# A graph network with mixtures of experts: gathers written out with their indices read from the table, and the first normalisation inside the stage that builds the masks

## The reference, cut to what matters

```python
x = x + _L0_gnn_ref(_layernorm(x), src, dst, ...)
# in each of two attention layers, 8 heads of 32:
e = sum(q[dst] * k[src]) / sqrt(32);  a = exp(e - segment_max(e, dst)[dst])
agg = segment_sum(v[src] * a / segment_sum(a, dst)[dst], dst)
h = _layer_norm(agg @ Wo + h, g, b)
x = x + _L0_ffn_ref(_layernorm(x)[None], ...)[0]
x = x + _L1_gnn_ref(_layernorm(x), W_self, W_neigh, src, dst)
# summed = segment_sum(h_sparse[src], dst);  h_self + summed / max(deg, 1)
x = x + _L1_ffn_ref(_layernorm(x)[None], ...)[0]
```

## Time and profile before

| | us |
|---|---|
| median of 3 runs | 6103.55 |
| lowest, highest | 6103.26, 6105.42 |
| the profiled execution | 6110.16 |
| its span, first to last instruction | 6108.3 |
| busy PE / DVE / ACT / POOL in the span | 4518.1 / 3914.2 / 2030.2 / 2849.7 |
| mean granted clock of PE, share of full speed | 0.884 |

### The profile page before, as it was taken

How to read it: one execution, slowest core, us unless ns; L and a number is a source line. 1 busy time by engine, 2 the same in 40 slices (tenths; PEclk the granted TensorE clock), 3 DMA queues, 4 the chain that set the end, 5 groups by cost and what they waited for, 6 DMA issues and landing times. The chain is left out here.

```text
span 6108.3 us, 95354 instructions
## 1 busy us (share of the span) xinstructions
PE 4518.1 (74%) x23436; PEld 3415.7 (56%) x23437; DVE 3914.2 (64%) x7196; ACT 2030.2 (33%) x4756; POOL 2849.7 (47%) x2776
## 2 busy tenths in 40 slices
PE   0589999999689999999859679364565656446986
PEld 0466666666476666666659679353443434424553
DVE  4668888888768888888766656795444444732332
ACT  0135555555415555555433223320000000213332
POOL 0057777777017777777300010006777777053332
PEclk9999999999899999999979889696777776557998
DMA  6457666666147666666420040013333333133334
GB/s 92 133 174 200 193 189 191 192 191 183 47 166 203 197 190 191 189 191 191 125 72 0 0 108 0 7 36 94 104 102 104 104 103 103 35 116 89 54 53 82
DMA packets 357896, 732.25 MB, mean 120 GB/s; under 512 B 73235, under 2 KB 205225, under 8 KB 357377
## 3 DMA queue, kind: packets, MB, share of 16 engines
q0 software_dynamic: 194912, 575.52, 34.3%
q1 hardware_dynamic: 162642, 150.27, 9.0%
q10 hardware_dynamic: 80, 3.20, 0.2%
HBM read 627.96 MB, written 107.19 MB: 120 GB/s over the span
## 5 line engine op out<-in xcount | busy, mean ns | idle before, releaser
L973 POOL DMA_INDIRECT rows_a<-kv_scratch,att_idx x848 | 862.5, 1017 | 923.6 <-issue 557.3
L735 POOL DMA_INDIRECT rows_a<-k_scratch,sage_sum_idx x832 | 802.9, 965 | 855.8 <-issue 850.9
L973 POOL DMA_INDIRECT rows_c<-kv_scratch,att_idx x816 | 878.7, 1077 | 268.6 <-issue 243.4
L1431 PE MATMUL ps<-rows_a 128*128 128x258 f32 x1664 | 626.6, 542 | 458.5 <-DMA rows_a<-k_scratch,sage_sum_idx 313.8
L1111 PE MATMUL ps<-attention_rows_b,att_work 128*128 x3328 | 848.0, 395 | 51.7 <-DVE att_work L1219 37.6
L1030 ACT ACTIVATE attention_rows_b<-ps x1664 | 649.3, 390 | 589.6 <-PE ps L1125 413.1
L1431 PEld LDWEIGHTS ps<-rows_a 128*128 128x128 f32 x1664 | 426.0, 268 | 658.7 <-DVE sage_rows_b L1409 394.4
L1409 DVE TENSOR_TENSOR sage_rows_b<-sage_rows_b,ps 128x258 f32 x832 | 353.1, 424 | 569.1 <-PE ps L1431 376.8
L1111 PEld LDWEIGHTS ps<-attention_rows_b,att_work 128*128 128x128 f32 x3328 | 596.6, 192 | 165.0 <-issue 91.2
L1125 PE MATMUL ps<-rows_a,att_work 128*128 128x264 f32 x1696 | 515.7, 431 | 63.2 <-issue 51.1
L1125 PE MATMUL ps<-rows_c,att_work 128*128 128x264 f32 x1632 | 504.8, 430 | 36.0 <-issue 30.2
(11 more groups left out here) (400 smaller groups left out, 9421.6 us busy)
## 6 DMA issues: line engine op xcount, KB each, us to landing
kv_scratch<-rows_c SPq DMA_DIRECT2D x100, 256.0 KB
slot_in<-rows_c SPq DMA_DIRECT2D x1, 13674.0 KB
rows_a<-slot_in SPq DMA_DIRECT2D x106, 129.0 KB
rows_a<-kv_scratch,att_idx POOLq DMA_INDIRECT x848
rows_a<-k_scratch,sage_sum_idx POOLq DMA_INDIRECT x832, 2.8
rows_c<-kv_scratch,att_idx POOLq DMA_INDIRECT x816
h_scratch<-rows_a SPq DMA_DIRECT2D x2, 6400.0 KB
rows_a<-h_scratch SPq DMA_DIRECT2D x50, 256.0 KB
```

What stands on the lines that cost most here:

```text
L735: pool.indirect_dma_start(ring[:, slot, 0:D], None, table, bass.IndirectOffsetOnAxis(ap=idx[:, slot:slot + 1], axis=0)).then_inc(landed[sl ...
L973: pool.indirect_dma_start(r.halves[h][:, u, 0:KV], None, c.kv_dram[:, :], bass.IndirectOffsetOnAxis(ap=idx[:, slot:slot + 1], axis=0)).the ...
L1431: mm = pe.matmul(c.ps[:, to:to + nw], s_buf[:, q, u, :], rhs, start=True, stop=True)
```

## The change

The load of `x` goes into the table stage, on ACT's queue, into `rows_c`. The masks' stage takes the statistics there and writes the normalised rows to `rows_a`; only then are the masks built over `x` in `rows_c`. The chain table is saved from ACT's queue. The masks' save is waited for at the end of the projection, with a semaphore that is held until attention is over; the projection's buffers in `rows_c` move behind the masks. `item_tile` moves to the end of `rows_b`. In attention and in the neighbour sums ACT's copies of indices are gone; POOL's gathers are written out, 104 halves of 8, each half with a wait on PE's count, and take their indices from `src_idx`.

```diff
-def item_tables(c, src, dst):
+def item_tables(c, x, src, dst):
...
+            @block.scalar
+            def _(a):
+                a.wait_ge(loaded, 96)
+                a.wait_ge(zeroed, 1)
+                rows = rows3(c.rows_c)
+                a.dma_start(rows[:, 0:FULL_ROWS // P, :],
+                            x[0:FULL_ROWS, :].rearrange("(t p) d -> p t d", p=P)).then_inc(x_loaded, 16)
+                a.dma_start(rows[0:LAST_ROWS, FULL_ROWS // P, :], x[FULL_ROWS:N, :]).then_inc(x_loaded, 16)
+                a.wait_ge(x_loaded, 32)
...
                 v.memset(st_i, 0).then_inc(padded, 1)
+                v.memset(c.rows_c[:, FULL_ROWS // P * D:NT * D], 0.0).then_inc(zeroed, 1)
...
# qkv
-        used_cols = [0]
+        used_cols = [BLOCKS * MASKW // 2]
...
                 sp.wait_ge(saved, 16)
+                sp.wait_ge(c.masks_saved, 16)
...
# segment_masks, SP
-                sp.wait_ge(zeroed, 1)
-                rows = rows3(c.rows_a)
-                sp.dma_start(rows[:, 0:FULL_ROWS // P, :],
-                             x[0:FULL_ROWS, :].rearrange("(t p) d -> p t d", p=P)).then_inc(x_loaded, 16)
-                sp.dma_start(rows[0:LAST_ROWS, FULL_ROWS // P, :], x[FULL_ROWS:N, :]).then_inc(x_loaded, 16)
                 sp.wait_ge(masked_all, 1)
-                sp.dma_start(c.mask_dram.rearrange("g p e -> p g e"), masks).then_inc(masks_saved, 16)
-                sp.wait_ge(row_ready, 1)
-                sp.dma_start(c.chain_dram.rearrange("(a i) -> a i", a=1), chain.rearrange("p b i -> p (b i)")
-                             ).then_inc(masks_saved, 16)
-                sp.wait_ge(x_loaded, 32)
-                sp.wait_ge(masks_saved, 32)
+                sp.dma_start(c.mask_dram.rearrange("g p e -> p g e"), masks).then_inc(c.masks_saved, 16)
+
+            @block.scalar
+            def _(a):
+                a.wait_ge(var_ready, 1)
+                a.activation(c.rstd[:, :], c.rstd[:, :], ACT.Sqrt).then_inc(rooted, 1)
+                a.wait_ge(scaled, 1)
+
+                def apply(t):
+                    at, col = bass.ds(t * D, D), bass.ds(t, 1)
+                    a.activation(c.rows_a[:, at], c.rows_c[:, at], ACT.Identity, bias=c.nbias[:, col],
+                                 scale=c.rstd[:, col]).then_inc(normed, 1)
+                tiles_of_ten(a, by_vector, NT - by_vector, apply)
+                a.wait_ge(row_ready, 1)
+                a.dma_start(c.chain_dram.rearrange("(a i) -> a i", a=1), chain.rearrange("p b i -> p (b i)")
+                            ).then_inc(chain_saved, 16)
+                a.wait_ge(chain_saved, 16)
...
# segment_masks, DVE
-                v.memset(c.rows_a[:, FULL_ROWS // P * D:NT * D], 0.0).then_inc(zeroed, 1)
...
                 do(v.tensor_scalar(c.head_mask[:, :], c.head_row[:, :], 1.0, BIG, ALU.subtract, ALU.mult))
+                tiles_of_ten(v, 0, NT, lambda t: row_stats(v, c, c.rows_c, t, taken))
+                v.wait_ge(taken, NT)
+                row_scales(v, c, do, var_ready, rooted, scaled)
...
+                tiles_of_ten(v, 0, by_vector, apply)
+                v.wait_ge(applied, by_vector)
+                v.wait_ge(normed, NT - by_vector)
                 v.wait_ge(loaded, 16 * (H + 1))
...
# attention, POOL
-                def fetch(i, h):
-                    pool.wait_ge(staged, i * RING_HALVES + h + 1)
+                for g in range(ITEMS // HALF):
+                    need(pool, summed, 8 * g - 40)
                     pool.sem_inc(gate, 1)
+                    h = g % RING_HALVES
                     for u in range(HALF):
-                        slot = h * HALF + u
+                        item = g * HALF + u
                         pool.indirect_dma_start(r.halves[h][:, u, 0:KV], None, c.kv_dram[:, :],
-                                                bass.IndirectOffsetOnAxis(ap=idx[:, slot:slot + 1], axis=0)
-                                                ).then_inc(landed[slot // BATCH], 16)
-                with pool.Fori(0, ROUNDS) as i:
-                    for h in range(RING_HALVES):
-                        fetch(i, h)
-                for h in range(ITEMS // HALF - ROUNDS * RING_HALVES):
-                    fetch(ROUNDS, h)
+                                                bass.IndirectOffsetOnAxis(ap=c.src_idx[:, item:item + 1], axis=0)
+                                                ).then_inc(landed[(h * HALF + u) // BATCH], 16)
...
# attention, ACT
-                def stage(g, n):
-                    need(a, summed, 8 * g - 40)
-                    a.activation(idx[:, n * HALF:(n + 1) * HALF], c.src_idx[:, bass.ds(g * HALF, HALF)],
-                                 ACT.Copy).then_inc(staged, 1)
...
# edge_sums, POOL (ACT's part is gone)
-                gather_rows(pool, table, ring, idx, staged, gate, landed, weighted)
+                for g in range(ITEMS // HALF):
+                    pool.wait_ge(summed, 2 * g + 2)
+                    pool.sem_inc(gate, 1)
+                    for u in range(HALF):
+                        item = g * HALF + u
+                        pool.indirect_dma_start(ring[:, item % RING, 0:D], None, table,
+                                                bass.IndirectOffsetOnAxis(ap=c.src_idx[:, item:item + 1], axis=0)
+                                                ).then_inc(landed[item % RING], 16)
...
# build
-            segment_masks(c, x)
-            layer_norm(c, c.rows_a, c.rows_a, "ln_in")
+            held = memory.enter_context(Semaphores(nc))
+            c.masks_saved = held.sem("masks_saved")
+            segment_masks(c)
```

More of the change, by code:

```diff
@@ L236, in item_tables @@
     bank_rows = c.rows_a[0:1, o:o + 3 * IC * P].bitcast(I32).rearrange("p (k i) -> p k i", k=3)
-    assert o + 3 * IC * P <= NT * D
+    assert o + 3 * IC * P <= NT * D and at[0] <= (NT + 1) * QW - IC * P
     with Semaphores(nc) as s:
@@ L429, in _ @@
                     v.wait_ge(taken, NT)
[L430 to L448, removed]
+                row_scales(v, c, do, var_ready, rooted, ready, normed_twice)
                 def apply(t):
@@ L773, in segment_masks @@
     with Semaphores(nc) as s:
-        loaded, step, zeroed, x_loaded = (s.sem(n) for n in ("sid_loaded", "mask_step", "pad_zeroed", "x_in_loaded"))
-        masked_all, masks_saved, row_ready, spread = (s.sem(n) for n in ("masked_all", "masks_saved", "cb_row", "cb_spread"))
+        loaded, step, chain_saved = (s.sem(n) for n in ("sid_loaded", "mask_step", "chain_saved"))
+        masked_all, row_ready, spread = (s.sem(n) for n in ("masked_all", "cb_row", "cb_spread"))
+        taken, var_ready, rooted, scaled, applied, normed = (
+            s.sem(f"ln_in_{n}") for n in ("stats", "var", "root", "ready", "applied", "normed"))
         with nc.Block() as block:
@@ L1051, in put_weights @@
                     a.activation(r.rescale, c.ps[:, X_PS + 384:X_PS + 384 + H], ACT.Copy).then_inc(r_ready, 1)
-                for h in range(RING_HALVES):
-                    stage(h, h)
                 for b in range(5):
@@ L1077, in phase @@
                             keep(g)
-                        if sums and q % 2 == 1 and within(i, RB, n - 3, 0, BATCHES - 2 * RING_HALVES):
-                            stage(blk * 2 + RING_HALVES - 1 + q // 2, (2 * k + RING_HALVES - 1 + q // 2) % RING_HALVES)
                 rounds(a, phase)
@@ L1353, in _ @@
                     pool.sem_inc(gate, 1)
-                gather_rows(pool, table, ring, idx, staged, gate, landed, weighted)
-            @block.scalar
-            def _(a):
-                free, per_batch = (msgs, 2) if weighted else (summed, 1)
-                for h in range(2):
-                    stage_indices(c, a, idx, staged, free, 0, h, per_batch)
-                with a.Fori(0, BATCHES // 4) as i:
-                    for q in range(4):
-                        if weighted:
-                            b = i * 4 + q
-                            a.wait_ge(summed, b + 1)
-                            a.activation(msg[:, q, :, D:SUMW],
-                                         c.scores[:, bass.ds(b * BATCH * H, BATCH * H)].rearrange("p (i h) -> p i h", h=H),
-                                         ACT.Copy).then_inc(weights, 1)
-                        if q % 2 == 0:
-                            stage_indices(c, a, idx, staged, free, i + 1, q // 2, per_batch)
+                for g in range(ITEMS // HALF):
[6 more added lines that the diff above has]
+                                                ).then_inc(landed[item % RING], 16)
             @block.vector
```

39 lines of the change are left out of this document (31 added, 8 removed).

## The result

| | before | after |
|---|---|---|
| median of 5 runs, us | 6103.26 | 6071.02 |
| lowest, highest | 6100.07, 6105.42 | 6064.35, 6072.69 |
| the profiled execution | 6110.16 | 6072.69 |
| its span | 6108.3 | 6070.6 |
| busy ACT / POOL | 2030.2 / 2849.7 | 1979.9 / 2863.6 |

The ratio is 0.9947, with a 95% interval of 0.9932 to 0.9961: 32 us faster, within 2.2 us of the forecast of 6068.8. The way there was not quite the one forecast: one term was too small, two others came to nothing, and one piece of the scatter was counted as gain.

A forecast was written before the change was run, and what follows sets the result against it. PE bounds attention, POOL the neighbour sums; in the beginning stages stand one behind another, so time saved there counts fully. 34 - 1 + 2 + 1 - 1.3 = 34.7 us gained, median 6068.8, range 6060 to 6086.

The forecast's parts named there:

- The normalisation, booked at nothing: Masks' stage: 29.5 us of normalisation fits DVE's idle time before the segment numbers land; ends about 131.2, nothing booked.
- cover and work are equal to within a microsecond: Masks' stage: DVE's idle 29.4 us (101.7 to 131.06) matches the normalisation's 29.5 us.
- The weights' use, 192: First projection: DVE uses its weights at 192 instead of 226.2, 34 us gained, ends 30.5 and 35.9.
- The gain is absolute: Whole kernel: the 34.7 us gain, found on the profiled execution, is taken off the median 6103.55, giving 6068.8.
- x's load, 1 us of loss: Table stage: x's load on ACT's queue may use up slack of SP's saves; 1 us lost, bounds 0 and 14.
- rival A: Table stage: x's load holds up SP's saves, POOL starts 2.8 to 14 us later; 6076, at most 6083; chance 0.26.
- Attention's start, 2 us: Attention: first gather leaves earlier without ACT's index copies; 1 us a layer, 2 us gained, bounds 0 and 5.
- an earlier start counts in full: Attention's start: DVE waited for three batches, so an earlier first gather counts in full up to about 2 us.
- Neighbour sums, 1 us: Neighbour sums: POOL's pace unchanged, one wait and the start get shorter; 1 us gained, bounds -4 and +2.
- rival B: Neighbour sums: POOL stops 1.5 us at each of 104 half rings, 153 us; 6222 us, slower; chance 0.05.
- The extra barrier, 1.3 us: End of attention: one more barrier for the held semaphore, 1.3 us lost.
- Rival C: Masks' stage: normalisation isn't covered, its 29.5 us go behind 131; 6098, no change that can be told; chance 0.05.

The follow-up runs named there:

- the gathers alone: Only the gather parts of the change (POOL waits on PE's count, indices from `src_idx`), on the kernel before: 6099.34 us, ratio 0.9996.
- the front alone: The change without its gather parts; attention and neighbour sums as in the kernel before, with ACT's index copies and loops: 6068.21 us, ratio 0.9945.
- the experiment without cover: The whole change, but DVE waits for the segment numbers ahead of the statistics of x: 6094.09 us, ratio 0.9984.
- the kernel with early loads: The change plus first projection's weights loaded in masks' stage and h stored by ACT; statistics and ACT's segment-number loads in table stage: 6053.99 us, ratio 0.9919.

## Why the prediction was right, step by step

**The normalisation, booked at nothing.** Right: the memset forecast at about 131.2 came at 131.56. The price of a lost cover, 29.5 us, was 26.3 at the weights' use (216.11) and 23 in the time. The step that cover and work are equal to within a microsecond failed: the cover was some 3 us short. In the profile this was made good in part by the tables, done 1.2 us earlier and not 1 us later, which is no more than such starts move by themselves.

**The weights' use, 192, with bounds 190.3 and 195.7.** The projection began where it was put (183.13 for about 183), but the use came at 189.78, and at 189.05 and 189.88 in two other profiles: under the lower bound. The term that failed is the weights' time behind the masks' save, 2.3 us at the least, after a save at 214 GB/s until 188. That rate was read from one profile, and a slow one: the same code needed 2.5 us less from save to statistics in the kernel with the gathers alone. In the changed kernel the same 24 us moved 240 GB/s, the weights among it; the save landed 23.4 us after its issue, at about 188 as booked, and the weights were used 1.9 us later (the second row lists a DMA: its line, queue, size, and us from issue to landing):

```profile
164.00:188.00 24.00, 2.63 (x10) 2.06 (x10) 11.41 (x22) 2.41 (x4) 0.00 (x0) 1.00 1.03 240
...
mask_scratch<-rows_c SPq DMA_DIRECT2D x1, 5018.0 KB, 23.4
```

so a part of the weights moved beside the last of the masks, not behind them, and they came about 2 us earlier than booked.

**From 34 us to the median.** "The gain is absolute" was the weak step. The profiled execution lay 6.6 us over the median, and the kernel with the gathers alone shows that some 4.4 us of such a difference can lie in the very stretch that the change shortens (226.17 against 221.76). Against 221.76 the gain at the weights is 32.0 us, which fits the 32.2 of the medians; two profiles of the old front are few, so this is an account that agrees and not a proof. By it the sum came within 2.2 us partly by luck, because errors cancelled: the use booked 2.2 us late, the base 4.4 us high, and 3 us of gain at the gathers that never came, against 1.6 us of loss booked too much (x's load, the barrier).

**x's load, 1 us of loss; rival A.** No loss that can be told, and A fell: POOL's first gather left at 23.0 to 23.6 in every kernel with x on ACT's queue, at 23.5 and 23.4 with the old front. By the rule of the Trainium skill that spoke for A, in Perfetto Trace Analysis, DMA Instruction — HWDGE (DVE, Sync), a generator shared by the issuing sequencers stays locked until a DMA's descriptors are all generated; this trace disagrees, with saves of 0.39 to 1.08 us on SP's queue inside the 15.98 us on ACT's. What did hold is that x's load held the next DMA of its own queue: 15.98 us there, 13.43 on SP's.

**Attention's start, 2 us.** Nothing. POOL's first gather left 0.7 us behind the stage's first memset instead of 2.3, and DVE's wait for gathers fell from 7.0 to 1.3 us, as forecast; but two steps failed. The delay is not the copies': it is 2.4 us in the gathers alone and 1.0 in the front alone, and in the second attention 1.0 with copies and 0.6 without, so the copies cost 0.3 us and most of the rest left with the old front, for a reason that no row names. And "an earlier start counts in full" failed too: in the changed kernel DVE waits there 10.3 us for PE (L1133), before 6.2. From the first memset of one attention to the first of the next the kernels with ACT's copies take 1457.2 and 1457.1 us, the changed one 1457.5 and 1458.1. PE sets the stage's pace, and a wait removed at its start became another engine's slack.

**Neighbour sums, 1 us; rival B.** The gaps stayed at 0.3, and B's stops did not come: one wait of 1.5 us, the other 41 on average no longer than the gap. The 1.8 us by which the sums are shorter than before (1054.7 for 1056.5) prove nothing, with 1049.2 and 1050.8 in kernels with either loop.

**The extra barrier, 1.3 us.** It costs 0.7. From the load of g for the layers' last normalisation to the first load of the next stage it is 37.31 us before and 38.01 after, in all kernels that hold the semaphore the same to 0.03 except the one with ACT's copies, 37.71:

```profile
3097.47 0.36 SPq L421 DMA_DIRECT2D layer_scores<-in_L_gnn_ln_g_dram  x1
...
3134.78 0.38 SPq L1732 DMA_DIRECT2D ffn_raw<-in_L_gnn_w_dram  x1
```

```profile
3064.79 0.37 SPq L455 DMA_DIRECT2D layer_scores<-in_L_gnn_ln_g_dram  x1
...
3102.80 0.38 SPq L1743 DMA_DIRECT2D ffn_raw<-in_L_gnn_w_dram  x1
```

**Rival C** was near: a cover 3 us short is a small C, and the experiment without cover gave its time, 6094 for 6098.

**Left open.** The second half of the last attention's output stage (from the load of x at 3063.03, L1478, to the load at 3097.47 shown above), which nobody edited, takes 34.4 and 35.3 us in the two profiles with the old front and 35.6 to 38.2 in all but one with the new. No row names a cause, and nothing was tried on it.

## What to carry to other kernels

Put work where its engine is idle, and measure both lengths, cover and work: here they agreed within 3 us, so nearly all of the 29 us stage vanished, and taking the work away on top of that brought nothing until the loads became faster too. When a difference of stretches is carried over to a median, ask in which stretch the profiled run was slow. A wait removed on an engine that doesn't set the stage's pace (POOL and ACT in attention) was worth nothing here, however plainly the trace showed it.

## What the runs showed of the hardware

Two queues carried these loads faster than one: eight loads of 416 KB, each into 16 partitions in pieces of 512 bytes, moved at 99 GB/s from one queue and at 184 from two, with the 16 engines' busy share shown as full in both. The Trainium skill, DMA: Bandwidth & Descriptors, Issuing engines are not separate DMA queues, says that issuing from several engines only saves issue time; for these loads the measurement decides otherwise, and DVE's wait fell from 22.46 to 9.37 us. Whether the queue or the 16 partitions of a load set the lower rate stays open; on one queue x's load, into 128 partitions in pieces of 1 KB, reached 348 GB/s.

A queue behind x's load held its own next DMA for 13.43 us (SP) and 15.98 us (ACT), and so the engine that issues it, while the other queue's DMAs went on. In the kernel with early loads ACT stood 37.19 us in eight issues, and DVE waited 14.94 us for its next activation. A load that is free in bytes can cost the engine that issues it.
